# Windowed attention, then Fourier mixing: layer-norm variances as four 64x64 products, PSUM banks given out anew

## The reference, cut to what matters

```python
a = _shifted_window_attention(x, qkv_w, qkv_b, proj_w, proj_b, logit_scale, ...)
x = x + _layernorm(a, norm1_g, norm1_b)
h = gelu(x @ fc1_w.T + fc1_b) @ fc2_w.T + fc2_b
x = x + _layernorm(h, norm2_g, norm2_b)
# layer 1: moving average + rfft, 128 modes x 128 modes per channel, irfft
```

## Time and profile before

| | |
|---|---|
| median of 3 runs | 8854.63 us (8853.43 to 8855.93) |
| the profiled execution | 8850.95 us |
| its span, first to last instruction | 8849.2 us |
| TensorE busy | 8401.3 us (95%) |
| ScalarE busy | 6230.1 us (70%) |
| VectorE, GpSimd busy | 5742.6 us (65%), 5155.6 us (58%) |
| granted TensorE clock, mean | 0.967 |

### The profile page before, as it was taken

One profiled execution on the slowest core, in us unless ns is written; L12 is line 12 of the kernel. 1 busy time (PEld: TensorE's weight loads), 2 busy tenths in 40 slices (PEclk: granted clock), 3 DMA queues, 4 the chain that ended last, 5 costly groups with the idle time before them and its releaser, 6 DMA issues.

```text
span 8849.2 us, 652880 instructions
## 1 busy us (share of the span) xinstructions
PE 8401.3 (95%) x291636; PEld 5471.0 (62%) x291636; DVE 5742.6 (65%) x8029; ACT 6230.1 (70%) x8530; POOL 5155.6 (58%) x5127
## 2 busy tenths in 40 slices
PE   8799999999999999999999999999999999878686
PEld 5556666666666666666666666666666666557565
DVE  1457777777777777777777777777777777222121
ACT  1468888888888888888888888888888888322121
POOL 0357777777777777777777777777777777100000
PEclk9789999999999999999999999999999999889888
DMA  3111111111111111111111111111111111699999
GB/s 99 39 32 38 37 38 38 38 38 37 38 38 38 38 38 37 38 37 35 36 38 37 38 38 38 38 37 38 38 38 38 37 37 36 202 324 319 337 317 332
DMA packets 1105192, 700.01 MB, mean 79 GB/s; under 512 B 616850, under 2 KB 1026834, under 8 KB 1100948
## 3 DMA queue, kind: packets, MB, share of 16 engines
q1 hardware_dynamic: 1100484, 564.33, 23.9%
q10 hardware_dynamic: 4608, 134.22, 3.5%
HBM read 412.97 MB, written 285.21 MB: 79 GB/s over the span
## 4 chain that ended last, share of the span: by engine, by line
PE 93%; DMA 4%; issue 1%; SPq 0%; POOL 0%; DVE 0%; ACTq 0%; ACT 0%; POOLq 0%; DVEq 0%
PE ps L475 15%; PE ps L453 13%; PE ps L511 12%; PE ps L523 11%; PE ps L436 10%; PE ps L551 10%; PE ps L501 6%; PE ps L487 5%; PE ps L495 5%; PE ps L424 3%; DMA out<-arena 3%; PE ps L398 1%; PE ps L389 1%; PE ps L390 1%; SPq L262 0%
## 5 line engine op out<-in xcount | busy, mean ns | idle before, releaser
L475 PEld LDWEIGHTS ps<-arena 32*32 32x32 f32 x131072 | 1290.9, 104 | 541.8 <-issue 508.4
L475 PE MATMUL ps<-arena 32*32 32x16 f32 x131072 | 1425.4, 186 | 17.9 <-issue 12.6
L664 ACT ACTIVATE arena<-ps,arena 128x1024 f32<-128x1024 f32 x1024 | 1140.4, 1114 | 357.8 <-PE ps L523 205.9
L775 DVE TENSOR_TENSOR arena<-ps,arena 128x768 f32<-128x768 f32 x1024 | 962.1, 940 | 539.3 <-PE ps L436 539.3
L913 POOL TENSOR_TENSOR arena<-arena 128x512 f32<-128x512 f32 x512 | 536.9, 1049 | 1282.9 <-DVE arena L846 1009.9
L453 PEld LDWEIGHTS ps<-arena 32*32 32x32 f32 x131072 | 1167.1, 105 | 152.6 <-issue 152.6
L453 PE MATMUL ps<-arena 32*32 32x16 f32 x131072 | 1218.9, 180 | 34.3 <-issue 34.3
L960 POOL TENSOR_TENSOR arena<-arena 128x512 f32<-128x512 f32 x512 | 629.5, 1230 | 1037.6 <-DVE arena L827 1037.6
L551 PE MATMUL ps<-xch,amat 128*128 128x256 f32 x4096 | 924.6, 388 | 288.0 <-ACT arena L688 214.3
L511 PE MATMUL ps<-arena 64*128 64x512 f32 x4096 | 1178.9, 652 | 8.6 <-ACT arena L664 4.5
L922 POOL TENSOR_TENSOR arena<-arena 128x512 f32<-128x512 f32 x1024 | 1044.0, 1041 | 10.5 <-PE ps L475 10.4
(11 more groups left out here) (89 smaller groups left out, 14021.8 us busy)
## 6 DMA issues: line engine op xcount, KB each, us to landing
arena<-in_x SPq DMA_DIRECT2D x4096, 32.0 KB
y<-ystripe SPq DMA_DIRECT2D x256, 512.0 KB, 5.3
amat<-mix SPq DMA_DIRECT2D x512, 256.0 KB, 3.4
xch<-y SPq DMA_DIRECT2D x512, 256.0 KB, 4.0
out<-arena ACTq DMA_DIRECT2D x32, 4096.0 KB, 27.1
mix<-amat SPq DMA_DIRECT2D x64, 256.0 KB, 2.0
wri<-in_w_real SPq DMA_DIRECT2D x64, 64.0 KB, 1.8
wri<-in_w_imag SPq DMA_DIRECT2D x64, 64.0 KB, 1.9
```

Of the source, the lines that this page charges most:

```text
L475: ins = mm(PV[32 * h:32 * h + 32, b, c0:c0 + N], vexp[r, sl, h, :, :], pT[r, sl, h // 2, h % 2, :], start=True, stop=True, tile_position=( ...
L664: f(hT[kk], M, ACT.Gelu, bias=b1[:, kk:kk + 1]).then_inc(done, 1)
L775: tt(qkv[ring(g, 4)][:, :, 4 * pp:4 * pp + 4, :].rearrange("p w s n -> p s w n"), M.rearrange("p a (s n) -> p (a s) n", s=2)[:, :, 0:3 * C ...
```

## The change

- The two variances of a step are computed together, in four products of 64x64 in the four quarters of the array: `sq2` in the quarters on the diagonal, `sq1` in the two others. For that the two halves of `sq1` must change places: SP copies them to `sq1x`, two transfers of 64 rows of 2 KB (128 KB each) per group. The step's one `variances` replaces `variance1` and `variance2`; it takes the squares of group i5 and of group i7.
- PSUM is given out anew: two pairs of banks, `MA` (0, 1) and `MB` (2, 3). `project_qkv` uses both, one per call, as does `first_layer`, and the variances use `MA`, the input's transpose the first bank of `MB`. The scores move into the free halves of the two banks of `PV` (4 and 5), so that `scores` now waits for `keep_o` of the same step (`oT_sb`).
- The lists of all engines are written out anew.

```diff
+                def variances(g, h):
+                    if there(g) or there(h):
+                        need(pe, sq1x_in, g, 32)
+                        need(pe, sq2_sb, h)
+                        after(pe, (qkvA_sb, i1), (gelu1, i7), (l1_sb, before(g), before(h)))
+                        settled(pe)
+                        for a in range(2):
+                            b = 1 - a
+                            ins = mm(V1[b * C:b * C + C, :], ones[a * C:a * C + C, a * C:a * C + C],
+                                     sq1x[a * C:a * C + C, :], start=True, stop=True, tile_position=(a * C, b * C))
+                        for a in range(2):
+                            ins = mm(V2[a * C:a * C + C, :], ones[a * C:a * C + C, a * C:a * C + C],
+                                     sq2[a * C:a * C + C, :], start=True, stop=True, tile_position=(a * C, a * C))
+                        ins.then_inc(var_ps, 1)
...
+            def swap_halves(g):
+                if there(g):
+                    need(sp, sq1_sb, g)
+                    for a in range(2):
+                        sp.dma_start(sq1x[a * C:a * C + C, :], sq1[(1 - a) * C:(2 - a) * C, :]).then_inc(sq1x_in, 16)
...
             with sp.Fori(2, NS // 2) as d:
                 for k in range(8):
                     load_x(d * 2 + k // GPS, k % GPS, Group(d * 8, k))
+                    swap_halves(Group(d * 8, k - SWAP))
                     if k % GPS == 0:
                         store_y(d * 2 + (k // GPS - 3), Group(d * 8, k - 12 + GPS - 1))
...
+        MA, MB = ps[:, 0:2, :], ps[:, 2:4, :]
+        PV = ps[:, 4:6, 0:256]
+        D1, H2 = ps[:, 6, :], ps[:, 7, :]
+        V1, V2 = MA[:, 0, :], MA[:, 1, :]
+        XT = MB[:, 0, :]
+        def S(sl):
+            return ps[:, 4 + sl // 4, 256:512]
...
 scores, part 0:
                             need(pe, qT_sb, g)
                             need(pe, kT_sb, g)
-                            need(pe, biased, before(g))
+                            after(pe, (oT_sb, i4), (biased, before(g)))
...
 first_layer, kk = 1:
-                            after(pe, (qkvB_sb, i0), (qkvA_sb, i0), (gelu0, i5), (gelu1, before(g)))
+                            after(pe, (l1_sb, i5, i7), (qkvA_sb, i1), (gelu1, before(g)))
...
 TensorE's list:
-                turn_x(i0); weighted(i4, 0); first_layer(i5, 0); weighted(i4, 1)
-                second_layer(i6, 0); second_layer(i6, 1); project(i4)
-                project_qkv(i0, 0); variance2(i6); variance1(i4); project_qkv(i0, 1)
-                scores(i2, 0); scores(i2, 1); first_layer(i5, 1)
+                project(i5); second_layer(i7, 0); second_layer(i7, 1)
+                project_qkv(i1, 0, MA); project_qkv(i1, 1, MB)
+                weighted(i4, 0); variances(i5, i7); first_layer(i6, 0, MB)
+                weighted(i4, 1); first_layer(i6, 1, MA)
+                scores(i2, 0); scores(i2, 1); turn_x(i0)
...
 ScalarE's list:
-                load EXP_SET; exponent(i4); log1(i5); log_norm(i2); root1(i5); log2(i7)
-                root_norm(i2); root2(i7); load GELU_SET; gelu(i6, 1); keep_x(i0)
-                square(i1); keep_o(i4); gelu(i5, 0); square2(i6); square1(i4)
+                load EXP_SET; log_norm(i2); root_norm(i2); square2(i7); exponent(i3)
+                log2(i7); log1(i5); root2(i7); root1(i5); load GELU_SET; keep_o(i4)
+                gelu(i6, 0, MB); square(i1); gelu(i6, 1, MA); square1(i4); keep_x(i0)
...
 VectorE's list:
+                qkv_out(i1, 1, MB); sum_prob(i3); turn_q(i2); invert(i3); turn_k(i2)
+                normed1(i5); add1(i5); normed2(i7); bias(i2); sum_squares(i1)
+                turn_prob(i3); maximum(i2); clamp(i1); qkv_out(i0, 0, MA); gain2(i7)
...
 GpSimd's list:
+                norm_k(i1); add2(i7); divide(i2); expand_v(i2); add_o1(i0)
+                add_o2(i4); shift(i1); scale_norm(i0); norm_q(i0)
```

More of the change, by code:

```diff
@@ L153, in swin_then_fourier @@
         oT = carve(512).rearrange("p (a s i) -> p a s i", a=2, i=N)
-        sq1, l1, r1, dn1, x1T = (carve(512) for _ in range(5))
+        sq1, sq1x, l1, r1, dn1, x1T = (carve(512) for _ in range(6))
         sq2, l2, r2, dn2, yg = (carve(512) for _ in range(5))
@@ L421, in turn_x @@
                         need(pe, x_in, g, 16 * 8)
-                        after(pe, (dn1_sb, i5), (xT_sb, before(g)))
+                        after(pe, (gelu0, i6), (qkvB_sb, i1), (xT_sb, before(g)))
                         for p in range(4):
@@ L464, in weighted @@
                             need(pe, v1_sb, g)
-                            after(pe, (l2_sb, i7), (oT_sb, before(g)))
+                            after(pe, (biased, i3), (oT_sb, before(g)))
                         else:
@@ L482, in project @@
                         need(pe, oT_sb, g)
-                        after(pe, (xT_sb, i0), (dn1_sb, before(g)))
+                        need(pe, dn1_sb, before(g))
                         d1 = D1.rearrange("p (s e n) -> p s e n", s=4, e=2)
@@ L628, in square1 @@
                         need(act, proj_ps, g)
-                        need(act, var1_ps, before(g))
+                        need(act, sq1x_in, before(g), 32)
                         f(sq1, D1, ACT.Square, bias=be1).then_inc(sq1_sb, 1)
@@ L645, in square2 @@
                         need(act, fc2b_ps, g)
-                        need(act, var2_ps, before(g))
+                        need_var(act, before(g))
                         f(sq2, H2, ACT.Square, bias=be2).then_inc(sq2_sb, 1)
@@ L650, in log2 @@
                     if there(g):
[L651 removed]
+                        need_var(act, g)
                         f(l2, V2, ACT.Ln, bias=eps).then_inc(l2_sb, 1)
@@ L658, in root2, with gelu @@
                         f(r2, l2, ACT.Exp, scale=-0.5).then_inc(r2_sb, 1)
-                def gelu(g, kk, ready, free, done):
+                def gelu(g, kk, M, ready, free, done):
                     if there(g):
@@ L666, in step @@
                 act.preload_act_table_set(EXP_SET)
-                exponent(i4)
+                log_norm(i2)
+                root_norm(i2)
+                square2(i7)
+                exponent(i3)
+                log2(i7)
                 log1(i5)
-                log_norm(i2)
+                root2(i7)
                 root1(i5)
-                log2(i7)
-                root_norm(i2)
-                root2(i7)
                 act.preload_act_table_set(GELU_SET)
-                gelu(i6, 1, fc1b_ps, fc2b_ps, gelu1)
-                keep_x(i0)
[L677 to L681, removed]
+                keep_o(i4)
+                gelu(i6, 0, MB, fc1a_ps, fc2a_ps, gelu0)
+                square(i1)
+                gelu(i6, 1, MA, fc1b_ps, fc2b_ps, gelu1)
+                square1(i4)
+                keep_x(i0)
             over_groups(act, step, 4)
@@ L768, in step, with qkv_out @@
                 i0, i1, i2, i3, i4, i5, i6, i7, i8 = ago(s, k)
-                def qkv_out(g, pp, ready, done):
+                def qkv_out(g, pp, M, ready, done):
                     if there(g):
```

120 lines of the change are left out of this document (59 added, 61 removed).

## The result

The changed kernel takes 10370.56 us, the median of 4 runs (10363.3 to 10374.27); the kernel before, run beside it, 8855.28 us (8853.43 to 8860.99). The ratio is 1.171, 95% interval [1.169, 1.173]: slower by 17%, far outside the predicted range. From here on "before" is 8855 us, or 8850.95 for its profiled execution.

What follows compares the result with a forecast made beforehand. The prediction took TensorE's own list to bound the kernel: 8851 - 553 (list) + 507 (stops before `scores`) + 124 (clock) = 8929 us, 8932 for the median of runs; range 8775 to 9160.

Steps and rivals of the forecast that it cites:

- TensorE's list, 12.90: TensorE's work in one loop step, start to start, falls from 13.98 to 12.90 us: 553 us off the kernel.
- Everything else keeps its shapes in another order, at no cost: TensorE's list: calls other than variances and qkv are only reordered and take no more time.
- The chain, 4.44: From the variances' end through ScalarE's logs, roots, table load and `keep_o` back to TensorE at `scores`: 4.44 us.
- The stop of 0.99: TensorE waits 0.99 us before `scores` for `keep_o` in every step: 507 us in the kernel.
- The step without the clock, 13.89: One loop step as list plus stop, 12.90 + 0.99 us, clock falls not counted: 8805 us for the kernel.
- rival 1: The granted clock stays at 1.00 in the loop: 8805 us, faster by 0.6%; chance 20%.
- SP and the swap, "Nothing": SP's queue: the swap lands 0.9 us before the variances need it, x loads in time; no cost.
- The clock, + 124: Stops before `scores` make the granted clock fall sometimes: 73 falls at 1.7 us each, 124 us.
- one step in seven: How often the stop before `scores` was to make the clock fall: 73 falls.
- Rival 4: The clock falls in every step, as in the ramp: 9675 us; chance 8%.
- Rival 3: In the variances only two quarters run at a time, 0.85 us more before log2: 9240 us; chance 10%.
- Rival 5: The swap lands after 5.6 us, too late for the variances; at a landing of 4.0 us, 9365 us; chance 5%.

Runs made afterwards that it cites:

- e5: The change with `keep_o` ahead of the Gelu table load and SP's stores of y ahead of the swap: 8544.5 us, ratio 0.965.
- e13: e9 without the swap, the variances by pairs in the two quarters on the diagonal: 8711.74 us, ratio 0.984.
- e7: The change with `first_layer`'s second half computed twice to fill the stop, and SP's stores ahead of the swap: 8988.24 us, ratio 1.015.
- e12: The change with only SP's stores of y moved ahead of the swap: 10362.29 us, ratio 1.171.
- e1: The change with `keep_o` moved ahead of the Gelu table load on ScalarE: 9005.28 us, ratio 1.018.
- e11: The change with the stop filled by a second pass of `weighted` (32x32 tiles), and SP's stores ahead of the swap: 10110.53 us, ratio 1.142.
- e4: e1 without the swap, both variances in the two quarters on the diagonal, one after the other: 8776.09 us, ratio 0.991.
- e6: e4 with `keep_o` behind the table load again: 10320.98 us, ratio 1.165.
- e9: e5 with the second `weighted` ahead of both `first_layer` halves, which then stand together: 8416.15 us, ratio 0.951.

## Why the prediction was wrong

By its own steps:

- **TensorE's list, 12.90.** The variances: 1.03 forecast, 1.02 measured (1.14 in the step behind). The two qkv together: 1.70 to 1.50, as forecast. "Everything else keeps its shapes in another order, at no cost" failed by 0.4 us: in e5, where no wait is listed, the step is 13.31 (`scores` at 5001.51 and 5014.82). `weighted` ahead of the variances takes 1.54 from start to start instead of 1.32, and `first_layer` ahead of `scores` 1.25 instead of 1.06. The second is `keep_o` again, through 0.25 us ahead of `scores` in e5 as in the change. The first was not tried by itself; it is there without the swap too (1.61 in e13).
- **The chain, 4.44.** Right in its order and nearly in its length, 4.60 us; the hand-over at its end was estimated at 0.13 and took 0.25. The stop of 0.99 was 1.04 in the step shown and 0.98 in the mean (171.9 us in 176 steps).
- **The step without the clock, 13.89.** e7 has it: 14.28, 8988 us. So rival 1 (8805, faster by 0.6%) would not have come true even at full clock. The 0.39 us are the 0.17 of the chain and the 0.23 of `weighted` ahead of the variances (5009.04 to 5010.60 in e7).
- **SP and the swap, "Nothing".** True for the change (e12: 8 us, within the spread). Wrong as soon as the step is short: the order on SP costs 461 us between e1 and e5. I had added the stores' own 1.4 us, but not that the eight loads behind them issue slower, 8.08 instead of 5.70.
- **The clock, + 124.** This is the step that failed. The frequency was put at "one step in seven", the price at 1.7 us, "nearer to never since the stop is shorter than any of the ramp's that a fall surely follows". It was every step and 2.80 us: 1434 us. Both factors were read too low from the same rows. The ramp had shown a fall behind 1.30 us of stop, and I took the length of the stop as the thing that decides; e11 has falls with no stop. The change's own falls come before `scores` starts, or at most 0.1 us behind its start, in all 176 steps. So if thin tiles have a part in them, it is those of `weighted` ahead of the stop; no run tried that by itself. And the shortest half-clock stretch of the ramp, 3.3 us, was taken as the price, though the other one in view had 10 us; here it is 6.8 us, and `scores`, which the prediction left out of what runs at half clock behind a fall, loses 1.29 us of the 2.80.
- **The rivals.** Rival 4, a fall in every step, was the case that came, at 8%. Its price of 9675 was too low for the same reason: 1.7 for 2.8 us per fall, and 0.4 us of list and chain. Rival 3 can be priced now: two quarters at a time take 0.84 more on TensorE (e4), and with the stop 10321 us (e6). Rival 5 did not come: no kernel's list has a wait of TensorE for the swap.

For the frequency the ramp held more than was read from it. The row taken in favour of few falls, 467.5 to 481.0, ends exactly where the clock falls; the next stretch of the same trace is

```profile
481.10:487.80 6.70, 5.66 (x133) 3.44 (x135) 2.85 (x4) 1.73 (x2) 4.84 (x5) 0.50 0.13 27
```

A stop of 1.10 us (at 473.6) did pass there without a fall. But between 436 and 590 no stretch at full clock lasted over 14 us, and only from 590.3 on, where TensorE no longer stops, is it 1.00, up to 7512.

The two sentences of the Trainium skill that were weighed (TensorE: Matmul & The Clock Gate, HAM oscillation) now stand apart. By its general rule a stop of one microsecond is too short to matter; these traces show the clock lost in every step behind 1.04 us, so here the measurement decides against it. The failure mode told behind it, short idles between groups of products, fits the change and e6. Neither sentence covers e11, where the clock falls with no idle time. That four 64x64 tiles are independent (TensorEngine Tiling, Tiling Modes) agrees with the trace: 1.02 us for all four.

The direction was right, and so was the first mechanism, the stop. But by the stop alone the kernel was to come out 46 us faster; that it is slower at all, and by how much, comes from the clock, which had been rated as a small addition.

## What to carry to other kernels

When a change puts a stop into a loop that ran without one, ask first what it does to the clock: the stop here cost 1.0 us, the fall of the clock with it 2.8. Don't go by the idle time alone: the same stop filled with thin products still let the clock fall (e11), filled with dense ones it did not (e7). The remedy can be one call: a copy that TensorE waits for belongs ahead of a table load, not behind it. And in an issuing queue keep what is due soonest ahead of, or well away from, large stores.

With these two repairs and one regrouping (e9) the changed kernel is 4.9% faster than the kernel before, of which the four quarters themselves bring 296 us (e13 to e9).

## What the runs showed of the hardware that was not expected

- The granted clock falls in e11 with TensorE busy for 99% of the time, a block of 32x32 tiles standing in the place of the stop (0.86), and holds at 1.00 in a kernel that idles 2% of the time (e7, busy 2940.59 of 3000 us).
- `scores`, 256 products of 16 columns, takes 3.55 us at 1.2 GHz and 2.29 at 2.4 GHz: these thin products lose less than half of their speed, but they do lose.
- Eight issues of x loads behind two stores on the same queue take 8.08 us, behind the swap 5.70.
- Four 64x64 tiles in the four quarters take 1.02 us for two passes of 512 columns; the same products in the two quarters of the diagonal 1.86.
